# Carrying per-pixel reciprocal deviations over a DRAM scratch, with square and norm on GpSimd

## The chip, the cores and the metric

The kernel runs on one core of a Trainium2 chip, as one launch. The metric is the device time of the whole program in microseconds. Before the change the median of three runs is 893.47 us (891.79 to 895.72).

## The reference

The input is x of shape (8, 64, 64, 64), batch, channel, row, column, in float32. Two blocks follow each other.

```
# block one: four scans; each line is the line before it, convolved over 9 taps and all channels
new = cur + relu(row_conv(prev, K))         # down, up, right, left

# block two
pooled = x.mean((2, 3)); hdn = layernorm(pooled @ w_fc1.T); dyn = hdn @ w_fc2.T   # a 5x5 filter per image and channel
out = depthwise_conv(x, dyn)                                    # 25 taps, zero padding
u = out.mean(1); s2 = square(out - u).mean(1)                   # over the 64 channels of a pixel
out = (out - u) * rsqrt(s2 + EPS); out = ln2_w * out + ln2_b
out = gelu(einsum(out, w_expand))                               # 64 -> 256 channels
gx = sqrt(sum(square(out), (2, 3))); nx = gx / (gx.mean(1) + EPS)
out = gamma * (out * nx) + beta + out
out = einsum(out, w_shrink) + x                                 # 256 -> 64 channels
```

## The kernel before

The function `scans` is block one. It keeps one line of all eight images on chip at a time and runs TensorE, VectorE and GpSimd in a serial chain, and it fills the first 500 us. Only two lines of it touch the change: it prepares the constants `pick` (L398, L399) and `spread` (L361 to L364), the second by one ScalarE copy.

The function `block_two` is block two. The image rows are folded on the partitions: partition c holds channel c of the even rows, partition 64 + c the same channel of the odd rows. An image is cut into two halves, so there are 16 units of 128 partitions by 16 row pairs by 64 columns, 1024 elements a partition.

Each engine has its own written-out order of instructions, a loop over slots s from -1 to 20, and the engines meet only through semaphores. In slot s:

- TensorE convolves unit s + 1 (`convolve`, L1043), in six pieces of five matmuls, into one of two pairs of PSUM banks. Five of the 15 tap pairs are its work. It also sums unit s - 1 over the channels (`statistics`, L1066), spreads the reciprocal deviations of unit s - 2 from rows of subtotals to all channels (`widen`, L1080, twice, each for half of the unit), expands that unit (`expand`, L1090, four times) and shrinks unit s - 5 (`shrink`, L1112, twice). `respond` (L1103) takes a mean over channels once for an image.
- VectorE adds ten taps of unit s onto the convolved sums in PSUM (`take_tap`, L872); the last one writes `inner` in SBUF. Between the taps stand `norm` (L902) of unit s - 2, `make_var` and `make_rstd` (L886, L896) of unit s - 1, `finish` (L932) of unit s - 5 and, once for an image, `sum_energy` and `respond` (L911, L915).
- ScalarE makes five products of unit s + 1 with its taps (`product`, L754), the square of `inner` (`square`, L766), the root of the variance (`root`, L779), the gelu of unit s - 2 (`gelu`, L791) and the sums of its squares (`add_squares`, L798).
- GpSimd sums the products into `part` (`add_product`, L711) and adds `part` to `inner` (`add_inner`, L718), splits the image for TensorE (`split_low`, L701) and builds the filter matrices of the next image (`make_dyn`, L724).
- SyncE issues the transfers: the rows that a tap needs from the other half of the partitions (`cross`, L670) and the stores of the output (`store`, L680).

`expand` waits for the gelu before it, since both use the one pair of banks `exp_ps`. A `statistics` writes the bank `stat_ps`, which `widen` uses as well. After the last taps (slot 16 and on) only expansion, gelu, shrinking and stores are left.

Of the kernel before, what the change touches and what calls it, by code (L numbers as in the profile page):

```python
# [64 lines left out]
def build(nc, x, k_td, k_dt, k_lr, k_rl, fc1, ln1_w, ln1_b, fc2, ln2_w, ln2_b,  # L65
          expand, shrink, gamma, beta, out):
    with ExitStack() as ctx:
# [4 lines left out]
        def sb(name, shape, dt=F32):  # L72
# [8 lines left out]
            pick=sb("pick", [P, 32 + 2 * SUBS - 2]),  # L81
# [10 lines left out]
            spread=sb("spread", [P, 4 * SUBS, P]),  # L92
# [6 lines left out]
def scans(nc, bank, kept, x, kernels, fc1, ln1_w, ln1_b, fc2, ln2_w, ln2_b,  # L99
# [6 lines left out]
    with ExitStack() as ctx:  # L106
# [181 lines left out]
        def _(act):  # L288
# [55 lines left out]
            with act.Fori(0, counts[1] // UNROLL) as i:  # L344
                for u in range(UNROLL):
# [15 lines left out]
            rows = ident[:, :].rearrange("p (g k) -> p g k", k=32)[:, :, 0:2 * SUBS].rearrange("p g (k a) -> p g k a", a=1)  # L361
            act.wait_ge(ident_ready, 1)
            act.activation(kept["spread"][:, :, :].rearrange("p (g j) (k c) -> p g (j k) c", j=SUBS, c=C),
                           rows.to_broadcast([P, 4, 2 * SUBS, C]), ACT.Copy)  # L364

# [4 lines left out]
        def _(dve):  # L370
# [25 lines left out]
            def prepare_constants():  # L396
                dve.wait_ge(consts, 1)
                dve.memset(kept["pick"][0:C, 2 * SUBS - 2:2 * SUBS - 1], 1.0 / C)  # L398
# [152 lines left out]
def block_two(nc, psum, kept, out):  # L551
# [4 lines left out]
    with ExitStack() as ctx:  # L556
# [10 lines left out]
        INNERS = 3  # L567
# [15 lines left out]
        normed = sb("normed", [P, 2, COLS])  # L583
# [17 lines left out]
        tap_lo = sb("tap_lo", [P, B, len(PE_TAPS), 2], F32R)  # L601

# [27 lines left out]
        wide_done = sem("wide_done")  # L630
# [29 lines left out]

        def out_bank(k):
            return out_ps if k < 4 * (B - 1) else psum[:, 4 + k % 4, :]
# [4 lines left out]
        def _(sp):  # L667
# [27 lines left out]
        def _(pool):  # L695
# [38 lines left out]

            pool.wait_ge(taps_known, 1)
            pool.wait_ge(dyn_ready, 1)
            for u in range(UNITS):
                for n in range(1, N_ACT):
                    add_product(u, n)
                if u + 2 < UNITS:  # L740
                    split_low(u + 2)
                if u % 2 == 0 and u // 2 + 1 < B:
                    make_dyn(u // 2 + 1)
                add_inner(u)

        @block.scalar
        def _(act):
# [18 lines left out]
            def square(u):  # L766
                act.wait_ge(inner_ready, u + 1)
                if u > 0:
                    act.wait_ge(stats_done, u)
                if u > 1:  # L770
                    act.wait_ge(energy_ready, 2 * (u - 1))
                act.activation(squares[:, :], inner[:, u % INNERS, :, :].rearrange("p j w -> p (j w)"),  # L772
                               ACT.Square).then_inc(squared, 1)

# [16 lines left out]
            def gelu(u, c, m):  # L791
                act.wait_ge(exp_done, 2 * (2 * u + c) + m + 1)
                if m == 0 and u >= WIDE:
                    act.wait_ge(out_done, 2 * (u - WIDE) + c + 1)
                act.activation(wide[:, m, :, u % WIDE, c * COLS:(c + 1) * COLS], exp_ps[:, :, :],  # L795
                               ACT.Gelu, bias=expand_bias[:, m:m + 1]).then_inc(gelu_done, 1)

            def add_squares(u, m):  # L798
                b, h = u // 2, u % 2
                act.wait_ge(gelu_done, 4 * (u + 1))  # L800
# [4 lines left out]
                if m == 0 and u + 1 < UNITS:  # L805
                    act.wait_ge(stats_done, u + 2)
                act.activation(squares[:, :].bitcast(BF16).rearrange("p (a n) -> p a n", a=2),
# [15 lines left out]
            for s in SLOTS_RUN:  # L823
                w, e, v = s - 1, s - 2, s - 5

                def products(lo, hi):
                    if s + 1 < UNITS:
                        for n in range(lo, min(hi, N_ACT)):
                            product(s + 1, (n + 1) % N_ACT)

                if 2 <= s + 2 < UNITS:
                    split_high(s + 2)
                for i in range(4):
                    if e in range(UNITS):
                        gelu(e, i // 2, i % 2)
                    products(i, i + 1)
                    if i == 1 and w in range(UNITS):
                        square(w)
                products(4, N_ACT)
# [3 lines left out]
                if 0 < e <= UNITS and e % 2 == 0:  # L843
                    root_energy(e // 2 - 1)
                if e in range(UNITS):
                    add_squares(e, 0)
                    add_squares(e, 1)

        @block.vector
        def _(dve):  # L850
# [21 lines left out]
            def take_tap(u, i):  # L872
# [6 lines left out]
                if i == N_DVE - 1 and u >= INNERS:  # L879
                    dve.wait_ge(normed_ready, 2 * (u - INNERS + 1))  # L880
# [15 lines left out]
            def make_rstd(u):  # L896
                dve.wait_ge(std_ready, u + 1)
                if u > 1:
                    dve.wait_ge(wide_done, 2 * (u - 1))
                dve.reciprocal(rstd[:, u % 2, :], std[:, :]).then_inc(rstd_ready, 1)  # L900

            def norm(u, c):  # L902
                k = 2 * u + c
                dve.wait_ge(wide_done, k + 1)
                if k >= 2:
                    dve.wait_ge(exp_done, 2 * k - 2)
                dve.tensor_tensor(normed[:, c, :],
                                  inner[:, u % INNERS, c * CROWS:(c + 1) * CROWS, :].rearrange("p j w -> p (j w)"),
                                  stat_ps[:, :], ALU.mult).then_inc(normed_ready, 1)
# [5 lines left out]
            def respond(b):  # L915
                n = RESP_STEPS * b
                dve.wait_ge(resp_mean, b + 1)
                dve.tensor_scalar(resp[:, 2, 0:1], out_ps[:, 0:1], EPS, None, ALU.add).then_inc(resp_step, 1)
# [62 lines left out]
            for s in SLOTS_RUN:  # L981
                w, e, v = s - 1, s - 2, s - 5
# [8 lines left out]
                if e in range(UNITS):  # L991
                    norm(e, 0)
                take(1)
# [3 lines left out]
                if e in range(UNITS):  # L997
                    norm(e, 1)
                take(2)
                if v >= 0:  # L1000
                    finish(v, 1)
                if 0 < e <= UNITS and e % 2 == 0:
                    sum_energy(e // 2 - 1)
                take(2)
# [6 lines left out]
                if 0 < e <= UNITS and e % 2 == 0:  # L1011
                    respond(e // 2 - 1)
# [3 lines left out]
        def _(pe):  # L1016
# [49 lines left out]
            def statistics(u):  # L1066
                pe.wait_ge(squared, u + 1)
                if u > 0:
                    pe.wait_ge(normed_ready, 2 * u)
                flat = inner[:, u % INNERS, :, :].rearrange("p j w -> p (j w)")  # L1070
                for n, image in enumerate((flat, squares)):
                    for k in range(SUBS):
                        for g in range(4):
                            at = (g * SUBS + k) * STAT_COLS
                            mm = pe.matmul(stat_ps[32 * g:32 * g + 32, n * STAT_COLS:(n + 1) * STAT_COLS],
                                           kept["pick"][:, 2 * (SUBS - 1 - k):2 * (SUBS - 1 - k) + 32],
# [3 lines left out]
            def widen(u, c):  # L1080
                pe.wait_ge(rstd_ready, u + 1)
                if c > 0:
                    pe.wait_ge(normed_ready, 2 * u + c)
                per = 2 * SUBS
                for g in range(per):
                    mm = pe.matmul(stat_ps[:, g * STAT_COLS:(g + 1) * STAT_COLS], kept["spread"][:, per * c + g, :],  # L1086
                                   rstd[:, u % 2, :], start=True, stop=True)
                mm.then_inc(wide_done, 1)

            def expand(u, c, m):  # L1090
                e = 2 * (2 * u + c) + m
                if m == 0:
                    pe.wait_ge(normed_ready, 2 * u + c + 1)
                if e > 0:
                    pe.wait_ge(gelu_done, e)
                else:
                    pe.wait_ge(weights_ready, 1)
                for hp in range(2):
                    half = slice(C * hp, C * hp + C)
                    mm = pe.matmul(exp_ps[:, hp, :], expand_w[half, m, :], normed[half, c, :], start=True, stop=True)  # L1100
                mm.then_inc(exp_done, 1)

            def respond(b):  # L1103
                pe.wait_ge(resp_root, b + 1)
                if b > 0:
                    pe.wait_ge(finished, 4 * b)
                for m in range(HALVES):
                    mm = pe.matmul(out_ps[:, 0:1], kept["mean_ce"][:, :].to_broadcast([P, P]), resp[:, 1, m:m + 1],
# [17 lines left out]
            for s in SLOTS_RUN:  # L1126
                u, w, e, v = s + 1, s - 1, s - 2, s - 5
# [5 lines left out]
                def at_w(stage, *which):  # L1133
                    if w in range(UNITS):
                        stage(w, *which)

                def at_e(stage, *which):
                    if e in range(UNITS):
                        stage(e, *which)

                def at_v(stage, *which):
                    if v >= 0:
                        stage(v, *which)

                at_e(widen, 0)
                at_v(shrink, 0)
                at_e(expand, 0, 0)
                conv(0)
                at_e(widen, 1)
                at_e(expand, 0, 1)  # L1150
                at_v(shrink, 1)
                at_e(expand, 1, 0)
                conv(1)
                at_e(expand, 1, 1)
                conv(2)
                at_w(statistics)
                conv(3)
                conv(4)
                if 0 < e <= UNITS and e % 2 == 0:
                    respond(e // 2 - 1)  # L1160
                conv(5)

# [25 lines left out]
```

## Time and profile before

| | |
|---|---|
| median of three runs | 893.47 us |
| the profiled execution | 893.85 us |
| its span | 892.0 us |
| TensorE matmuls | 816.9 us, 92% of the span |
| VectorE | 604.4 us, 68% |
| GpSimd | 454.5 us, 51% |
| ScalarE | 433.2 us, 49% |
| mean granted TensorE clock | 0.97 of full speed |

The page cuts the span into 40 slices; two of its lines show the two blocks. The busy shares over the whole span are a mean over both, and block two (from the 23rd slice on) has other shares than block one.

```
PE   5999999999999999999999675889999999999775
ACT  5690005777750000000000154798989898988662
```

A time in the answers is counted from the start of the span. "busy" is the time of the instructions, and an idle time is put down to the instruction that ended it.

### The profile page before, as it was taken

How to read it: one execution, taken by the hardware profiler on the slowest of the kernel's cores; microseconds unless marked ns; L12 is line 12 of the kernel's file. 1: busy time of each engine (PE TensorE's matmuls, PEld its weight loads, DVE VectorE, ACT ScalarE, POOL GpSimd, SP SyncE). 2: the span in 40 equal slices, each digit the busy share in tenths (PEclk: the TensorE clock that was granted, in tenths of full speed). 3: DMA queues.
4: the chain of work that ended last, by engine and by line, in shares of the span. 5: the costliest groups of instructions: out<-in, count | busy, mean ns of one | idle time of the engine just before them, and what ended most of it. 6: DMA issues, size and time to landing. Idle time of an engine off the chain costs nothing. (4 is left out here: it accounts for less than half of the span.)

```text
span 892.0 us, 16129 instructions
## 1 busy us (share of the span) xinstructions
PE 816.9 (92%) x5639; PEld 666.5 (75%) x5639; DVE 604.4 (68%) x1127; ACT 433.2 (49%) x520; POOL 454.5 (51%) x443
## 2 busy tenths in 40 slices
PE   5999999999999999999999675889999999999775
PEld 5999999999999999999999654455454555545231
DVE  4666666666666666678888657777887778888722
ACT  5690005777750000000000154798989898988662
POOL 2333333333323333368888466767777776765500
PEclk9999999999999999999999788889999999999997
DMA  6750000000000000000000100110222222223123
GB/s 139 170 141 0 0 0 1 0 0 0 0 1 1 0 0 0 1 1 0 0 0 0 47 0 24 34 36 24 48 47 47 47 47 47 47 47 71 24 48 71
DMA packets 51189, 26.99 MB, mean 30 GB/s; under 512 B 40720, under 2 KB 49104, under 8 KB 51152
## 3 DMA queue, kind: packets, MB, share of 16 engines
q1 hardware_dynamic: 51152, 26.51, 13.2%
q8 instruction: 22, 0.36, 0.2%
q14 instruction: 15, 0.12, 0.0%
HBM read 9.98 MB, written 8.39 MB: 21 GB/s over the span
## 5 line engine op out<-in xcount | busy, mean ns | idle before, releaser
L487 PE MATMUL psum<-line_hi,taps_hi 128*128 128x256 f32 x1270 | 203.0, 292 | 11.8 <-DVE taps_lo L383 8.6
L501 PE MATMUL psum<-line_lo,taps_hi 128*128 128x256 f32 x1270 | 202.5, 291 | 0.8 <-DVE line_lo L436 0.8
L495 PE MATMUL psum<-line_hi,taps_lo 128*128 128x256 f32 x1270 | 202.0, 291 | 0.0
L436 DVE SCALAR_TENSOR_TENSOR line_lo<-psum,rest 128x256 fp32r<-128x256 f32 x254 | 108.2, 426 | 123.6 <-POOL rest L263 115.3
L487 PEld LDWEIGHTS psum<-line_hi,taps_hi 128*128 128x128 f32 x1270 | 177.1, 192 | 13.0 <-issue 9.3
L501 PEld LDWEIGHTS psum<-line_lo,taps_hi 128*128 128x128 f32 x1270 | 176.4, 191 | 2.0 <-DVE line_lo L436 1.8
L495 PEld LDWEIGHTS psum<-line_hi,taps_lo 128*128 128x128 f32 x1270 | 176.7, 191 | 0.0
L263 POOL TENSOR_TENSOR rest<-x,line_hi 128x256 f32<-128x256 f32 x127 | 82.9, 653 | 168.5 <-DVE line_hi L427 168.5
L709 POOL TENSOR_TENSOR part<-part,prod 128x960 f32<-128x960 f32 (+2 forms) x64 | 145.2, 2269 | 24.3 <-ACT part L764 17.5
L315 ACT ACTIVATE by_h<-x (+1 forms) x128 | 85.7, 670 | 106.1 <-DVE x L416 104.5
L263 POOL TENSOR_TENSOR rest<-by_h,line_hi 128x256 f32<-128x256 f32 x127 | 91.5, 721 | 83.4 <-DVE line_hi L427 83.4
L416 DVE TENSOR_TENSOR x<-line_hi,line_lo 128x256 f32 (+1 forms) x190 | 105.5, 555 | 0.2
L883 DVE SCALAR_TENSOR_TENSOR psum<-x,tap_all,psum 128x930 f32<-128x930 f32 (+2 forms) x80 | 96.7, 1209 | 1.3
L1100 PE MATMUL psum<-normed,expand_w 64*128 64x512 f32 x256 | 75.0, 663 | 22.6 <-ACT wide L795 17.1
L764 ACT ACTIVATE prod<-x,tap_all 128x960 f32<-128x960 f32 (+2 forms) x64 | 70.1, 1101 | 37.5 <-POOL part L709 30.1
L883 DVE SCALAR_TENSOR_TENSOR psum<-crossed,tap_cross,psum 128x992 f32<-128x992 f32 (+1 forms) x64 | 80.7, 1261 | 10.3 <-PE psum L1060 9.4
L722 POOL TENSOR_TENSOR inner<-inner,part 128x1024 f32<-128x1024 f32 x16 | 37.9, 2367 | 86.5 <-DVE inner L883 86.5
L795 ACT ACTIVATE wide<-psum,expand_bias 128x1024 f32<-128x1024 f32 x64 | 70.9, 1109 | 20.9 <-PE psum L1100 20.7
L1060 PE MATMUL psum<-x_hi,dyn_hi 128*128 128x512 f32 x160 | 70.3, 439 | 9.1 <-DVE inner L883 5.8
L751 ACT ACTIVATE x_hi<-x 128x1024 fp32r<-128x1024 f32 x16 | 16.7, 1051 | 126.2 <-PEq L106 121.7
L1121 PE MATMUL psum<-wide,shrink_now 128*64 128x512 f32 x256 | 67.1, 653 | 3.7 <-DVE shrink_now L928 2.9
L427 DVE SCALAR_TENSOR_TENSOR line_hi<-psum,x 128x256 fp32r<-128x256 f32 x127 | 54.0, 425 | 21.9 <-PE psum L487 8.6
(129 smaller groups left out, 899.3 us busy)
## 6 DMA issues: line engine op xcount, KB each, us to landing
stage<-in_x_dram SPq DMA_DIRECT2D x32, 256.0 KB, 4.1
out_dram<-x SPq DMA_DIRECT2D x32, 256.0 KB, 4.4
crossed<-x SPq DMA_DIRECT2D x16, 256.0 KB, 3.5
crossed<-x SPq DMA_DIRECT2D x16, 240.0 KB, 3.6
fc_in<-in_L_conv_w_fc_dram SPq DMA_DIRECT2D x2, 100.0 KB
taps<-in_L_conv_k_td_dram SPq DMA_DIRECT2D x2, 80.0 KB, 3.3
taps<-in_L_conv_k_dt_dram SPq DMA_DIRECT2D x2, 80.0 KB, 3.3
taps<-in_L_conv_k_lr_dram SPq DMA_DIRECT2D x2, 80.0 KB, 3.5
```

The lines of the kernel that those rows point to most:

```text
L263: pool.tensor_tensor(rest[:, slot % 2, :].rearrange("p (b i) -> p b i", b=B), x_line, line_hi[:, (slot + 1) % SLOTS, :, REACH:REACH + WP]. ...
L315: act.activation(dst, src, ACT.Copy).then_inc(turned, 1)
L416: dve.tensor_tensor(kept_line(s, row_of(s, k)), line_hi[:, made, :, part].bitcast(F32), line_lo[:, made, :, part].bitcast(F32), ALU.add).t ...
L436: dve.scalar_tensor_tensor(out=line_lo[:, (slot + 1) % SLOTS, :, part], in0=as_lines(line_ps[slot][:, 0:LINE]), scalar=0.0, in1=as_lines(r ...
L487: mm = pe.matmul(line_ps[slot][:, 0:LINE], taps_hi[:, s, d, :], line_hi[:, slot, :, d:d + WP], start=(d == 0), stop=(d == OFFSETS - 1))
L495: pe.matmul(line_ps[slot][:, 0:LINE], taps_lo[:, s, d, :], line_hi[:, slot, :, d:d + WP], start=False, stop=False, skip_group_check=True)
L501: mm = pe.matmul(line_ps[slot][:, 0:LINE], taps_hi[:, s, d, :], line_lo[:, slot, :, d:d + WP], start=False, stop=(d == OFFSETS - 1), skip_ ...
L709: pool.tensor_tensor(dst, dst, other, ALU.add).then_inc(part_step, 1)
L795: act.activation(wide[:, m, :, u % WIDE, c * COLS:(c + 1) * COLS], exp_ps[:, :, :], ACT.Gelu, bias=expand_bias[:, m:m + 1]).then_inc(gelu_ ...
L883: dve.scalar_tensor_tensor(out=dst, in0=src, scalar=weight, in1=here, op0=ALU.mult, op1=ALU.add).then_inc(tap_step, 1)
L1060: mm = pe.matmul(conv_ps[:, 2 * (u % 2) + c, :], weight[:, b % 2, n, :, :].rearrange("p o c -> p (o c)"), image[:, u % 2, CROWS * c:CROWS ...
L1100: mm = pe.matmul(exp_ps[:, hp, :], expand_w[half, m, :], normed[half, c, :], start=True, stop=True)
```

## The change

The products on ScalarE become four and the taps on VectorE eleven: the tap ("up", 3) moves. `widen` and the constant `spread` go. In their place SyncE stores the reciprocal deviations of a unit in DRAM and reads them back twice, each time broadcast to 64 partitions, into `rstd_wide`. `square` moves from ScalarE to GpSimd, and `norm` from VectorE to GpSimd, one instruction for a unit where there were two. `inner` has two buffers in place of three, `normed` holds two whole units. `add_squares` writes to a buffer of its own, `dump`. The expansion goes by channel halves first (m) and image halves second (c), and for the last two units it uses three pairs of banks. The order of the slots changes on all engines.

```
-            ("down", 3), ("cross", 2)]
+            ("down", 3), ("up", 3), ("cross", 2)]
-SIDES = [("up", 1), ("down", 1), ("up", 3)]
+SIDES = [("up", 1), ("down", 1)]
-        INNERS = 3
+        INNERS = 2
+        EXP_SETS = 3
+        FREE_CONV = 4 * (UNITS - 2)
+        def exp_set(e):
+            first = 4 if e < FREE_CONV else (4, 0, 2)[(e - FREE_CONV) % EXP_SETS]
+            return psum[:, first:first + 2, :]
# SyncE
+            def spread_rstd(u):
+                sp.wait_ge(rstd_ready, u + 1)
+                if u > 1:
+                    sp.wait_ge(rstd_spread, 32 * (u - 1))
+                sp.dma_start(rstd_dram[u % 2], rstd[:, u % 2, :]).then_inc(rstd_stored[u % 2], 16)
+                sp.wait_ge(rstd_stored[u % 2], 16 * (u // 2 + 1))
+                if u > 0:
+                    sp.wait_ge(normed_ready, u)
+                rows = rstd_dram[u % 2].rearrange("(g q) n -> g (q n)", g=4)
+                for h in range(2):
+                    mine = rows[:, SUBS * h * STAT_COLS:SUBS * (h + 1) * STAT_COLS].rearrange("(a g) n -> a g n", a=1)
+                    sp.dma_start(rstd_wide[C * h:C * h + C, :].rearrange("p (g n) -> p g n", g=4),
+                                 mine.to_broadcast([C, 4, SUBS * STAT_COLS])).then_inc(rstd_spread, 16)
             for s in SLOTS_RUN:
+                if s - 1 in range(UNITS):
+                    spread_rstd(s - 1)
+                if s >= 5:
+                    store(s - 5)
                 if s + 2 < UNITS:
                     cross(s + 2)
-                if s >= 5:
-                    store(s - 5)
# GpSimd
+            def square(u):
+                pool.wait_ge(inner_ready, u + 1)
+                if u > 0:
+                    pool.wait_ge(stats_done, u)
+                pool.tensor_tensor(squares[:, :], image, image, ALU.mult).then_inc(squared, 1)
+            def norm(u):
+                pool.wait_ge(rstd_spread, 32 * (u + 1))
+                if u > 1:
+                    pool.wait_ge(exp_done, 4 * (u - 1))
+                pool.tensor_tensor(normed[:, u % 2, :], image, rstd_wide[:, :], ALU.mult).then_inc(normed_ready, 1)
-            for u in range(UNITS):
-                (add_product x4, split_low, make_dyn, add_inner of unit u)
+            for s in range(UNITS + 2):
+                w, e = s - 1, s - 2
+                if w in range(UNITS):
+                    add_inner(w)
+                    square(w)
+                if e >= 0:
+                    norm(e)
+                if s < UNITS:
+                    for n in range(1, N_ACT):
+                        add_product(s, n)
+                if s + 2 < UNITS:
+                    split_low(s + 2)
+                if s % 2 == 0 and s // 2 + 1 < B:
+                    make_dyn(s // 2 + 1)
# ScalarE, in a slot (n = s - 3)
+                add_squares(n, 1); split_high(s + 2); product(s + 1, 0)
+                square_mean(w); root(w)
+                if n in range(UNITS) and n % 2 == 1: root_energy(n // 2)
+                gelu(e, 0, 0); product(s + 1, 1); product(s + 1, 2); gelu(e, 0, 1); add_squares(e, 0)
+                gelu(e, 1, 0); product(s + 1, 3); gelu(e, 1, 1)
# VectorE, in a slot
+                take(2); finish(v, 0); take(2)
+                if n in range(UNITS) and n % 2 == 1: sum_energy(n // 2)
+                make_var(w); take(1); make_rstd(w); take(1); finish(v, 1); take(1)
+                if n in range(UNITS) and n % 2 == 1: respond(n // 2)
+                take(N_DVE)
# TensorE, in a slot
+                shrink(v, 0); conv(0); conv(1); statistics(w); expand(e, 0, 0); shrink(v, 1)
+                conv(2); expand(e, 0, 1); conv(3)
+                if n in range(UNITS) and n % 2 == 1: respond(n // 2)
+                expand(e, 1, 0); conv(4); conv(5); expand(e, 1, 1)
```

The lists of the three engines are written here one call after the other; in the kernel each stands under the test that its unit exists. `expand` now waits for the gelu before it only up to the last two units.

## Rows read from the trace of the kernel before

**Rows 1.** Timeline of GpSimd, `add_inner`: start us, us, engine, line, operation [idle before].
```profile
537.88 2.37 POOL L722 TENSOR_TENSOR inner<-inner,part 128x1024 f32<-128x1024 f32 x1 [3.13 <-DVE inner L883]
...
619.55 2.37 POOL L722 TENSOR_TENSOR inner<-inner,part 128x1024 f32<-128x1024 f32 x1 [5.31 <-DVE inner L883]
...
639.38 2.38 POOL L722 TENSOR_TENSOR inner<-inner,part 128x1024 f32<-128x1024 f32 x1 [5.95 <-DVE inner L883]
...
660.17 2.37 POOL L722 TENSOR_TENSOR inner<-inner,part 128x1024 f32<-128x1024 f32 x1 [4.63 <-DVE inner L883]
...
822.65 2.36 POOL L722 TENSOR_TENSOR inner<-inner,part 128x1024 f32<-128x1024 f32 x1 [9.02 <-DVE inner L883]
838.82 2.35 POOL L722 TENSOR_TENSOR inner<-inner,part 128x1024 f32<-128x1024 f32 x1 [4.33 <-DVE inner L883]
```

**Rows 2.** Windows: stretch, length, busy of PE, PEld, DVE, ACT, POOL, clock, DMA.
```profile
639.39:802.00 162.61, 154.50 (x900) 84.46 (x896) 130.39 (x161) 147.73 (x157) 116.85 (x57) 1.00 0.24 52
```

**Rows 3.** Groups by form, 640 to 802 us: busy us, mean ns | idle before, releaser.
```profile
L722 POOL TENSOR_TENSOR inner<-inner,part 128x1024 f32<-128x1024 f32 x9 | 21.4, 2374 | 48.3 <-DVE inner L883 48.3
...
L704 POOL TENSOR_TENSOR x_lo<-x,x_hi 128x1024 fp32r<-128x1024 f32 x8 | 16.0, 2005 | 0.0
...
L907 DVE TENSOR_TENSOR normed<-inner,psum 128x512 f32<-128x512 f32 x16 | 10.9, 680 | 0.0
...
L900 DVE RECIPROCAL rstd<-std 128x128 f32<-128x128 f32 x8 | 7.6, 953 | 0.0
...
L891 DVE TENSOR_TENSOR var<-psum,mean_sq 128x128 f32<-128x128 f32 x8 | 2.3, 292 | 30.4 <-ACT mean_sq L777 30.4
```

**Rows 4.** Groups of the page, whole span: a cross tap and a gelu.
```profile
L883 DVE SCALAR_TENSOR_TENSOR psum<-crossed,tap_cross,psum 128x992 f32<-128x992 f32 (+1 forms) x64 | 80.7, 1261 | 10.3 <-PE psum L1060 9.4
...
L795 ACT ACTIVATE wide<-psum,expand_bias 128x1024 f32<-128x1024 f32 x64 | 70.9, 1109 | 20.9 <-PE psum L1100 20.7
```

**Rows 5.** Timeline of one slot, 700 to 722 us.
```profile
705.78 1.94 PE L1121 MATMUL psum<-wide,shrink_now 128*64 128x512 f32 x8
...
707.65 1.13 PE L1100 MATMUL psum<-normed,expand_w 64*128 64x512 f32 x4
...
708.71 0.51 PE L1060 MATMUL psum<-x_hi,dyn_lo 128*128 128x512 f32 x1
...
713.40 0.64 PE L1075 MATMUL psum<-inner,pick 128*32 128x128 f32 x16
...
714.41 0.50 PE L1060 MATMUL psum<-x_hi,dyn_hi 128*128 128x512 f32 x1
...
715.46 1.28 ACT L783 ACT_TABLE_LOAD   x1
...
718.20 1.16 PE L1086 MATMUL psum<-rstd,spread 128*128 128x128 f32 x8
```

**Rows 6.** Timeline of TensorE: groups that began after an idle time.
```profile
578.23 2.07 PE L1100 MATMUL psum<-normed,expand_w 64*128 64x512 f32 x4 [1.86 <-DVE normed L907]
585.61 1.13 PE L1100 MATMUL psum<-normed,expand_w 64*128 64x512 f32 x4 [1.31 <-ACT wide L795]
```

**Rows 7.** Windows of 1 us: the granted clock stands before the last two numbers.
```profile
580.00:581.00 1.00, 1.00 (x4) 0.67 (x3) 0.96 (x2) 0.99 (x2) 1.00 (x2) 0.50 0.70 234
```

**Rows 8.** Timeline of a slot with `respond`, 818 to 822 us.
```profile
818.33 0.60 PE L1108 MATMUL psum<-resp,mean_ce 128*128 128x1 f32 x4 [0.25 <-ACT resp L789]
...
820.18 0.15 DVE L918 TENSOR_SCALAR resp<-psum 128x1 f32<-128x1 f32 x1
...
821.24 1.27 DVE L883 SCALAR_TENSOR_TENSOR inner<-crossed,tap_cross,psum 128x1024 f32<-128x1024 f32 x1
```

**Rows 9.** DMA issues: operation, count, KB each, us to landing.
```profile
crossed<-x SPq DMA_DIRECT2D x16, 256.0 KB, 3.5
```

**Rows 10.** Timeline of the end: the last sum of squares, the last shrinking.
```profile
870.92 1.91 ACT L807 ACTIVATE squares<-wide 128x2048 bf16<-128x2048 f32 x1
...
876.33 9.91 PE L1121 MATMUL psum<-wide,shrink_now 128*64 128x512 f32 x32 [1.23 <-DVE shrink_now L928]
```

More of the change, by code:

```diff
@@ L823, in _ @@
             for s in SLOTS_RUN:
[L824 to L829, printed above, removed]
+                w, e, n = s - 1, s - 2, s - 3
+                if n in range(UNITS):
+                    add_squares(n, 1)
                 if 2 <= s + 2 < UNITS:
                     split_high(s + 2)
[L833 to L839, printed above, removed]
+                if s + 1 < UNITS:
+                    product(s + 1, 0)
                 if w in range(UNITS):
@@ L842, in _ @@
                     root(w)
[L843 to L847, printed above, removed]
+                if n in range(UNITS) and n % 2 == 1:
+                    root_energy(n // 2)
+                for i, between in enumerate(((1, 2), (), (3,), ())):
+                    if e in range(UNITS):
+                        gelu(e, i // 2, i % 2)
+                    if i == 1 and e in range(UNITS):
+                        add_squares(e, 0)
+                    for p in between:
+                        if s + 1 < UNITS:
+                            product(s + 1, p)
         @block.vector
@@ L989, in take @@
                     taken[0] += n
-                if e in range(UNITS):
-                    norm(e, 0)
-                take(1)
+                take(2)
                 if v >= 0:
@@ L996, in _ @@
                 take(2)
[L997 to L1004, printed above, removed]
+                if n in range(UNITS) and n % 2 == 1:
+                    sum_energy(n // 2)
                 if w in range(UNITS):
@@ L1010, in _ @@
                 take(1)
-                if 0 < e <= UNITS and e % 2 == 0:
-                    respond(e // 2 - 1)
+                if v >= 0:
+                    finish(v, 1)
+                take(1)
+                if n in range(UNITS) and n % 2 == 1:
+                    respond(n // 2)
                 take(N_DVE)
@@ L1075, in statistics, with expand @@
                             mm = pe.matmul(stat_ps[32 * g:32 * g + 32, n * STAT_COLS:(n + 1) * STAT_COLS],
-                                           kept["pick"][:, 2 * (SUBS - 1 - k):2 * (SUBS - 1 - k) + 32],
+                                           kept["pick"][:, SUBS - 1 - k:SUBS - 1 - k + 32],
                                            image[:, at:at + STAT_COLS], start=(k == 0), stop=(k == SUBS - 1))
                 mm.then_inc(stats_done, 1)
[L1080 to L1094, printed above, removed]
+            def expand(u, m, c):
+                e = 4 * u + 2 * m + c
+                if e == 0:
+                    pe.wait_ge(weights_ready, 1)
+                if c == 0 and m == 0:
+                    pe.wait_ge(normed_ready, u + 1)
+                if e == FREE_CONV + 1:
+                    pe.wait_ge(tap_step, N_DVE * UNITS)
+                if 0 < e <= FREE_CONV:
                     pe.wait_ge(gelu_done, e)
-                else:
-                    pe.wait_ge(weights_ready, 1)
+                elif e >= FREE_CONV + EXP_SETS:
+                    pe.wait_ge(gelu_done, e - EXP_SETS + 1)
                 for hp in range(2):
                     half = slice(C * hp, C * hp + C)
-                    mm = pe.matmul(exp_ps[:, hp, :], expand_w[half, m, :], normed[half, c, :], start=True, stop=True)
+                    mm = pe.matmul(exp_set(e)[:, hp, :], expand_w[half, m, :], normed[half, u % 2, c * COLS:(c + 1) * COLS],
+                                   start=True, stop=True)
                 mm.then_inc(exp_done, 1)
@@ L1131, in conv, with at_e, at_v @@
                         convolve(u, piece)
[L1133 to L1137, printed above, removed]
+                def at_e(m, c):
                     if e in range(UNITS):
-                        stage(e, *which)
-                def at_v(stage, *which):
+                        expand(e, m, c)
+                def at_v(c):
                     if v >= 0:
[L1143 to L1147, printed above, removed]
+                        shrink(v, c)
+                at_v(0)
                 conv(0)
[L1149 to L1152, printed above, removed]
                 conv(1)
-                at_e(expand, 1, 1)
+                if w in range(UNITS):
+                    statistics(w)
+                at_e(0, 0)
+                at_v(1)
                 conv(2)
-                at_w(statistics)
+                at_e(0, 1)
                 conv(3)
+                if n in range(UNITS) and n % 2 == 1:
+                    respond(n // 2)
+                at_e(1, 0)
                 conv(4)
-                if 0 < e <= UNITS and e % 2 == 0:
-                    respond(e // 2 - 1)
                 conv(5)
+                at_e(1, 1)
 _INS = ['x', 'L0_conv_k_td', 'L0_conv_k_dt', 'L0_conv_k_lr', 'L0_conv_k_rl', 'L1_conv_w_fc1', 'L1_conv_ln1_w',
```

70 lines of the change are left out of this document (23 added, 47 removed).

## The prediction

> **What bounds the kernel now.** First the slices of the page: block two begins at about 500 us, and the change touches nothing before it but a ScalarE copy that lies in an idle stretch. Then the timeline of `add_inner`, which GpSimd starts when VectorE has finished the taps of a unit, so the distance of two of them is a slot [rows 1]. A slot with an odd number takes 639.38 - 619.55 = 19.83 us, an even one, which also carries `respond`, 660.17 - 639.38 = 20.79. Slots 1 to 4 take 81.67 us, slots 5 to 14 203.10 (five odd, five even), slot 15, the last with taps, 16.17, and what follows 892.0 - 838.82 = 53.2.
>
> Next the windows of eight steady slots (162.6 us) [rows 2]. For one slot of 20.3 us TensorE is busy 19.3, ScalarE 18.5, VectorE 16.3, GpSimd 14.6. Two engines are nearly full. VectorE idles 3.8 us a slot in one place, where `make_var` waits for the squared mean [rows 3]: the square of `inner` stands in the middle of ScalarE's list and `statistics` behind it on TensorE. So the period is a loop through all four engines, and not one engine's sum.
>
> **The change, part by part, for one steady slot.**
>
> TensorE: `widen` goes, two groups of eight, 1.16 us each with the last one's tail [rows 5], about 1.05 without it; 19.3 becomes 17.2. ScalarE loses a product (1.1) and the square (1.0): 16.4. VectorE loses two `norm` (0.68 each [rows 3]) and gains a tap (1.26 [rows 4]): 16.2. GpSimd loses an addition (2.2 to 2.37, as `inner`'s) and gains a square and a norm. The trace has no multiplication of two full images on GpSimd; the nearest row is its addition of the same 128 by 1024 shape, 2.37 us [rows 3]. I take 2.37 for each. Bounds: 2.0 (the subtraction of `split_low`, same shape [rows 3]) and 3.1 (a third over the addition). That makes 14.6 - 2.3 + 4.7 = 17.0. The four engines now stand at 16.2 to 17.2, so the sums alone would allow 17.2; what follows is the walk through the waits.
>
> Walk, with time 0 where VectorE starts the taps of slot s and GpSimd its list 0.14 later. Starts that follow each other on one engine are a little closer than the durations, and I use these: shrink 1.87, expand 1.07 (the steps 705.78, 707.65, 708.71), fifteen convolution matmuls in 718.20 - 714.41 = 3.79, so 1.26 a piece, statistics 1.01 [rows 5]; tap 1.25 and gelu 1.1 [rows 4], `add_squares` 1.9 [rows 10], reciprocal 0.95 [rows 3], and `finish`, of `norm`'s size but with a third operand, 0.72.
> - GpSimd: inner until 2.5, square until 4.8, norm until 7.2.
> - TensorE: the pieces 0 and 1 of the convolution are done before 4.8, or at 5.5 where TensorE comes late; statistics until 5.9 (6.5); expand from 7.2 to 8.3, shrink to 10.1, piece 2 to 11.4, expand to 12.5, piece 3 to 13.75, then `respond` in even slots, expand, pieces 4 and 5, done at 17.5 to 17.8, and the last expand until 18.9.
> - ScalarE: squared mean at 6.2 (6.8), table load 1.28 [rows 5], root until 7.9 (8.4), table load, first gelu from 9.7 to 10.9, two products to 12.9, gelu to 14.0 (TensorE's third expand waits for it, 0.2 us), `add_squares` to 15.9, gelu to 17.0, product, gelu after the last expand.
> - VectorE: two taps, `finish`, two taps until 5.8; variance at 6.3 (6.8) instead of after a wait of 3.8 us; then two taps, reciprocal, `finish`, a tap: 12.6; the last four taps take 4.9.
>
> *Odd slots.* VectorE is through at 17.4, and TensorE's convolution, which gates the next taps, at 17.5. But TensorE now idles from 2.9 to 4.9, since it has come to `statistics` before GpSimd has the square. After an idle 1.86 us the first group of four took 2.07 us in place of 1.13, after 1.31 us it did not [rows 6], and two microseconds behind the first the granted clock is 0.50, the lower level, 1.2 GHz [rows 7]. Idle here is about 1.95 us, so I take the fall: statistics takes 1.8, the variance starts at 7.0, and the slot ends at 17.9 (17.4 without it). Against 19.83 that is 1.9.
>
> *Even slots.* VectorE comes to `respond` at 12.8, but TensorE makes the mean only behind piece 3, at 14.35 (13.75 and 0.60). In the trace TensorE starts it at 818.33 and VectorE, which had other work, spends 821.24 - 820.18 = 1.06 us on its five small steps before the next tap [rows 8]. So VectorE waits 1.5 us: 14.4, 15.5, and four taps: 20.4. Against 20.79 that is 0.4. This wait is what takes the place of the old one: behind it on VectorE stand four taps, and GpSimd and the convolution after next wait for these.
>
> *The scratch.* In slot s - 1 the reciprocal is ready at 9.6; GpSimd comes to the norm at 17.9 + 4.8 = 22.7. Between lie three transfers on SyncE's queue, one after the other and two together. The trace has no store to a scratch; the nearest row is the shifted copy, 256 KB in 3.5 us [rows 9]. With issues of 0.6 each I take 3.6 + 4.2 = 7.8 us; bounds 4 (half a copy for each hop) and 12 (the copies behind one another and behind a store). It is hidden by 5 us in the steady part and costs in full in the tail. The Trainium skill, page "DMA: Bandwidth & Descriptors", section "Anatomy of one DMA — SWDGE (gpsimd) path", has 2.0 us of fixed cost for each transfer, most of it the receipt of the write, and bytes over 436 GB/s. No run here shows a store of 64 KB; by the page, as an estimate, the bounce would be 2.15 + 3.2 = 5.4 us, and the tail 2.4 us shorter than I make it.
> SyncE's wait for `rstd_ready` stands ahead of `store` and `cross`. The store goes behind the second `finish` (11.6) anyway, `cross` behind the last tap, with a slot to land in: nothing.
>
> *Start.* Slot 0 has only taps: +1.2. Slots 1 to 4: the first ends at 16.6 by VectorE (variance at 6.3, seven taps, reciprocal), the second and third at 17.75 (no shrink yet, TensorE reaches the third expand before its gelu, and pieces 4 and 5 end at 17.7), slot 4 at 20.0 (`respond` behind piece 3 at 13.9). Together 72.1 against 81.67: -9.6.
>
> *Slots 5 to 14.* 5 x 17.9 + 5 x 20.4 = 191.5 against 203.1: -11.6.
>
> *Slot 15.* No convolution, so the slot was short before; the new order has eleven taps and the wait for GpSimd's square at the lower clock: 17.95 against 16.17: +1.8.
>
> *Tail.* Before, 876.33 - 838.82 = 37.5 us lie between the start of slot 16 and the last shrinking, 3.4 of it behind the last sum of squares (870.92, 1.91 and 0.1 to read its result) [rows 1, 10]. Now: reciprocal at 9.6, bounce to 17.4, norm to 19.8, expand at the lower clock to 21.9, gelu, shrink and expand to 26.3, gelu, one `add_squares`, two gelus until 31.5, the last `add_squares` to 33.4, and 3.4: 36.8. The three pairs of banks save about what the scratch costs: -0.7.
>
> Sum: +1.2 - 9.6 - 11.6 + 1.8 - 0.7 = -18.9. On the profiled execution, 893.85, that is 874.95; this one lies 0.4 above the median, so 874.6 there. I say 875.
>
> **The rivals.**
>
> A. *TensorE is the last everywhere.* The lower clock also holds through the first expand of even slots, or GpSimd's square and norm take 2.8 each. For it: the first expand is reached by a chain of three GpSimd instructions at 7.2 with nothing to spare. Against: the idle before it is 0.7 to 1.3 us, and 1.31 kept the clock [rows 6]. 0.8 us later in each slot: pairs of 39.6 us instead of 40.6, -5 in slots 5 to 14, -6.4 in 1 to 4, the rest as above (+2.3): -9.1, so 884.8.
>
> B. *The clock stays, and the scratch is fast.* Odd slots end at 17.4 (-2.6 in all), and each hop takes under 3 us, -2.5 in the tail: 869.8.
>
> C. *ScalarE takes the gain.* Its two table loads, the root and the gelus form a chain that must start behind `statistics`; if each gelu is reached about 1.5 us later than in my walk, the third expand waits for it and the pieces behind it too. For it: the third expand already waits 0.2 us. Against: ScalarE's sum falls by 2.1. Pairs stay at 40.6, slots 1 to 4 give 4, the rest +2.3: 892.
>
> D. *Slower: the scratch comes late.* From the reciprocal at 9.6 of one slot to the tap behind the next convolution there are the bounce, norm 2.4 and 10.6 of TensorE; two slots last at least 22.6 us and the bounce. With a bounce over 18 us a pair is longer than the 40.6 of before: broadcasting one 4 KB piece of DRAM to 64 partitions would have to crawl, or stand behind stores. At 19.5 us: pairs of 42.1, +7.5 in slots 5 to 14, +3 in slots 1 to 4, +12 in the tail, +3 in slots 0 and 15: 919. Nothing in the row of 3.5 us speaks for it.
>
> That the change does not do what it says would mean that VectorE still waits at the variance; only with the square late on GpSimd, which is A.
>
> **How the numbers follow.** Forecast 0.50, A 0.18, B 0.17, C 0.10, D 0.05. The predicted time is that of the forecast. Two in ten may be left out: D, most of C, and a little of B and A; 866 to 887. No change here means within 0.5%, 889.0 to 897.9, which is about what a measurement of this kernel tells apart: C and little else, 0.09. Slower: D and the worst of C, 0.06. Faster 0.85.
>
> **What would show it.** Distances of `add_inner` near 17.9 and 20.4 in turn; the idle before `make_var` down from 3.8 us to under 1.5; a new idle on VectorE of about 1.5 us ahead of `respond` in even slots, put down to TensorE; clock 0.50 behind `statistics` in odd slots only; the norm on GpSimd never waiting for a transfer before slot 17, and there for about 10 us. The forecast is wrong if even slots are as short as odd ones, if GpSimd waits for `rstd_wide` in the steady part, or if the square takes 3 us or more.

## The result, and the profile after

The changed kernel takes 888.32 us, median of nine runs (884.66 to 889.81), against 893.44 us before. The ratio is 0.9932, 95% interval 0.9915 to 0.9949. The profiled execution took 888.81 us with a span of 887.1. It is faster, as forecast, but by 0.7% where 2.1% were forecast, and 888.3 lies outside the range of 866 to 887.

The timeline of GpSimd in the changed kernel, `add_inner` (now L744; start us, us), shows from slot 8 on slots in turn of 23.5 (even) and 17.6 us (odd), where 20.8 and 19.8 stood before [rows 1]. Slot 5 takes 19.55 and slot 7 16.86:

```profile
539.73 2.37 POOL L744 TENSOR_TENSOR inner<-inner,part 128x1024 f32<-128x1024 f32 x1 [8.25 <-DVE inner L910]
...
697.44 2.38 POOL L744 TENSOR_TENSOR inner<-inner,part 128x1024 f32<-128x1024 f32 x1 [5.33 <-DVE inner L910]
...
715.04 2.37 POOL L744 TENSOR_TENSOR inner<-inner,part 128x1024 f32<-128x1024 f32 x1 [1.96 <-DVE inner L910]
...
738.50 2.38 POOL L744 TENSOR_TENSOR inner<-inner,part 128x1024 f32<-128x1024 f32 x1 [5.33 <-DVE inner L910]
...
797.04 2.37 POOL L744 TENSOR_TENSOR inner<-inner,part 128x1024 f32<-128x1024 f32 x1 [1.86 <-DVE inner L910]
...
817.73 2.36 POOL L744 TENSOR_TENSOR inner<-inner,part 128x1024 f32<-128x1024 f32 x1 [6.64 <-DVE inner L910]
836.56 2.35 POOL L744 TENSOR_TENSOR inner<-inner,part 128x1024 f32<-128x1024 f32 x1 [5.20 <-DVE inner L910]
```

Slot 14 (797.04 to 817.73) is even too, and takes only 20.69. The groups by form, 640 to 802 us, say what is dear in the others (busy us, mean ns | idle before):

```profile
L762 POOL TENSOR_TENSOR squares<-inner 128x1024 f32<-128x1024 f32 x8 | 15.2, 1895 | 0.6
...
L946 DVE TENSOR_TENSOR shrink_now<-shrink_t,resp 128x128 f32<-128x128 f32 x4 | 5.2, 1308 | 0.1
...
L943 DVE TENSOR_SCALAR resp<-resp 128x2 f32<-128x2 f32 x4 | 4.8, 1193 | 0.1
...
L940 DVE SCALAR_TENSOR_TENSOR resp<-resp,gamma 128x2 f32<-128x2 f32 x4 | 3.4, 850 | 0.1
...
L918 DVE TENSOR_TENSOR var<-psum,mean_sq 128x128 f32<-128x128 f32 x8 | 2.3, 292 | 6.8 <-ACT mean_sq L810 6.8
...
L938 DVE RECIPROCAL resp<-resp 128x1 f32<-128x1 f32 x4 | 0.7, 164 | 0.1
L936 DVE TENSOR_SCALAR resp<-psum 128x1 f32<-128x1 f32 x4 | 0.6, 158 | 6.6 <-PE psum L1116 6.6
```

The wait at the variance went from 3.8 to 0.85 us a slot [rows 3], and the new wait ahead of `respond` is 1.65 us, both as forecast. But three of the five steps of `respond`, on 2 or 128 elements a partition, take 0.85, 1.19 and 1.31 us. Before the change the same view gave them 221, 170 and 293 ns. GpSimd's timeline of the same even slot suggests a cause, which the experiments test; first VectorE, then GpSimd:

```profile
688.60 0.16 DVE L938 RECIPROCAL resp<-resp 128x1 f32<-128x1 f32 x1
688.80 0.89 DVE L940 SCALAR_TENSOR_TENSOR resp<-resp,gamma 128x2 f32<-128x2 f32 x1
689.73 1.19 DVE L943 TENSOR_SCALAR resp<-resp 128x2 f32<-128x2 f32 x1
690.95 1.31 DVE L946 TENSOR_TENSOR shrink_now<-shrink_t,resp 128x128 f32<-128x128 f32 x1
```

```profile
687.67 2.00 POOL L726 TENSOR_TENSOR x_lo<-x,x_hi 128x1024 fp32r<-128x1024 f32 x1
689.63 1.26 POOL L753 TENSOR_TENSOR dyn_hi<-ident_half,tap_hi 128x640 fp32r<-128x640 f32 x1
690.86 1.26 POOL L753 TENSOR_TENSOR dyn_lo<-ident_half,tap_lo 128x640 fp32r<-128x640 f32 x1
```

Each slow step ends when a GpSimd instruction ends: 689.69 and 689.67, 690.92 and 690.89, 692.26 and 692.12. By then GpSimd has begun its next instruction, and the next step waits for that one. In slot 14 GpSimd has no image to split and no filters to build; its list is through, and the same three steps take their old times:

```profile
811.80 0.22 DVE L940 SCALAR_TENSOR_TENSOR resp<-resp,gamma 128x2 f32<-128x2 f32 x1
812.05 0.17 DVE L943 TENSOR_SCALAR resp<-resp 128x2 f32<-128x2 f32 x1
812.25 0.29 DVE L946 TENSOR_TENSOR shrink_now<-shrink_t,resp 128x128 f32<-128x128 f32 x1
```

The theory (called L in the experiments) is that VectorE and GpSimd exclude each other at SBUF for these forms of instruction. The Trainium skill states it: page "SBUF — State Buffer", section "SBUF: two separate sides", has a port pair shared by the two and held for a whole instruction, by any GpSimd operation, and on VectorE by one in a two-port mode or, against a GpSimd operation that reads SBUF, by one with two SBUF inputs. The rival (M) is that the steps are slow because of the scratch's transfers, or because a wait is counted as busy time.

### The profile page after: what moved, and what is told of

Its sections match the earlier page's. It is cut to its first block and busy times, and to the rows that moved or that the text cites. A ratio compares the mean times of both kernels' runs of the same rounds, so it can differ in the third digit from the quotient of the medians.

```text
span 887.1 us, 15588 instructions
## 1 busy us (share of the span) xinstructions
PE 797.9 (90%) x5383; PEld 643.8 (73%) x5383; DVE 620.0 (70%) x1111; ACT 399.6 (45%) x485; POOL 485.9 (55%) x459
## 5 line engine op out<-in xcount | busy, mean ns | idle before, releaser
L731 POOL TENSOR_TENSOR part<-part,prod 128x960 f32<-128x960 f32 (+2 forms) x48 | 108.6, 2262 | 20.9 <-ACT prod L806 16.0
L910 DVE SCALAR_TENSOR_TENSOR psum<-x,tap_all,psum 128x930 f32<-128x930 f32 (+3 forms) x96 | 116.4, 1213 | 1.7
L1107 PE MATMUL psum<-normed,expand_w 64*128 64x512 f32 x256 | 77.3, 686 | 23.3 <-POOL normed L769 11.7
L1073 PE MATMUL psum<-x_hi,dyn_hi 128*128 128x512 f32 x160 | 72.7, 455 | 24.5 <-DVE inner L910 21.1
L744 POOL TENSOR_TENSOR inner<-inner,part 128x1024 f32<-128x1024 f32 x16 | 38.0, 2372 | 61.4 <-DVE inner L910 61.4
L1073 PEld LDWEIGHTS psum<-x_hi,dyn_hi 128*128 128x128 f32 x160 | 33.1, 207 | 52.2 <-DVE inner L910 26.3
L1073 PE MATMUL psum<-x_lo,dyn_hi 128*128 128x512 f32 x160 | 70.1, 438 | 0.0
```

What stands on the lines that cost most here:

```text
L731: pool.tensor_tensor(dst, dst, other, ALU.add).then_inc(part_step, 1)
L910: dve.scalar_tensor_tensor(out=dst, in0=src, scalar=weight, in1=here, op0=ALU.mult, op1=ALU.add).then_inc(tap_step, 1)
L1073: mm = pe.matmul(conv_ps[:, 2 * (u % 2) + c, :], weight[:, b % 2, n, :, :].rearrange("p o c -> p (o c)"), image[:, u % 2, CROWS * c:CROWS ...
L1107: mm = pe.matmul(exp_set(e)[:, hp, :], expand_w[half, m, :], normed[half, u % 2, c * COLS:(c + 1) * COLS], start=True, stop=True)
```

## Experiments

**1. `respond` with its operands in PSUM.** Same five steps in the same places; gamma is copied once to two spare columns. `...` stands for what is left out of a line.

```
+            at = 2 * STAT_COLS + 8 + HALVES * i          # resp_ps(i): columns of the statistics bank
-  scalar_tensor_tensor(out=resp[:, 4, :], in0=resp[:, 1, :], ..., in1=kept["gamma"][:, :], ...)
-  tensor_scalar(resp[:, 5, :], resp[:, 4, :], 1.0, None, ALU.add)
-  tensor_tensor(shrink_now, kept["shrink_t"], resp[:, 5, :]..., ALU.mult)
+  scalar_tensor_tensor(out=resp_ps(1), in0=resp[:, 1, :], ..., in1=resp_ps(0), ...)
+  tensor_scalar(resp_ps(2), resp_ps(1), 1.0, None, ALU.add)
+  tensor_tensor(shrink_now, kept["shrink_t"], resp_ps(2)..., ALU.mult)
```

> The changed kernel with the operands of VectorE's respond in PSUM: gamma, the product and the sum with 1 lie in spare columns of the statistics bank, so that no step of it has two SBUF inputs or goes from SBUF to SBUF. Theory L (port): in the changed kernel three of the five steps took 0.85, 1.19 and 1.31 us on the mean where they took 0.22, 0.17 and 0.29 before, because VectorE stands still until the GpSimd instruction in flight has ended; with PSUM operands they go back to 0.15 to 0.35 each, even slots shrink from 23.5 to about 20.8 us, and the program by about 7 slots of 2.7 us: 866 to 873. Theory M (the steps are slow for the DMA traffic of the scratch or for a wait that the profile counts as busy): they stay near 1 us, time unchanged at 888.

Measured: 871.42 us, ratio to before 0.9752 (0.9723 to 0.9781). The groups by form, 640 to 802 us:

```profile
L950 DVE TENSOR_TENSOR shrink_now<-shrink_t,psum 128x128 f32<-128x128 f32 x5 | 1.4, 288 | 0.2
L944 DVE SCALAR_TENSOR_TENSOR psum<-resp,psum 128x2 f32<-128x2 f32 x5 | 1.1, 224 | 0.2
...
L940 DVE TENSOR_SCALAR resp<-psum 128x1 f32<-128x1 f32 x5 | 0.8, 158 | 8.2 <-PE psum L1121 8.2
```

The steps are back at 0.29 and 0.22 us, the even slots 8, 10 and 12 take 20.7 (slot 6 takes 21.0, slot 4 22.6), and 16.9 us are gained on the changed kernel. The scratch's transfers and the waits between the steps are all still there. Slot 14, where nothing was stalled, keeps its time (20.75 and 20.69), so PSUM operands as such give nothing. So M does not hold.

**2. TensorE's `respond` one place earlier**, ahead of `expand(e, 0, 1)` and piece 3.

> The changed kernel with TensorE's respond one place earlier, behind piece 2 of the convolution instead of behind the expand and piece 3. The mean then comes about 2.3 us earlier, before VectorE reaches its respond. My step 'VectorE waits 1.5 us there' says: the idle before VectorE's respond goes from 1.65 to near 0 and even slots from 23.5 to about 21.9; if the port theory holds, the three slow steps may come out longer or shorter, depending on which GpSimd instructions they now meet (they are then beside the additions of products). 876 to 882. The rival, that the wait for TensorE is not on the path: 888.

Measured: 879.99 us, 0.9847 (0.9821 to 0.9874). The wait is gone (no idle ahead of the first step), and even slots take 22.2. The three steps came out longer, 0.72, 1.93 and 1.31 us on the mean: in all 0.6 us more than in the changed kernel. The first one still meets an addition of products, but it is the middle one that grows, since it now meets the 2.00 us of `split_low` (first VectorE, then GpSimd):

```profile
682.87 0.72 DVE L940 SCALAR_TENSOR_TENSOR resp<-resp,gamma 128x2 f32<-128x2 f32 x1
683.62 1.94 DVE L943 TENSOR_SCALAR resp<-resp 128x2 f32<-128x2 f32 x1
```

```profile
683.53 2.00 POOL L726 TENSOR_TENSOR x_lo<-x,x_hi 128x1024 fp32r<-128x1024 f32 x1
```

Not all odd slots gained: 7 and 9 take 18.5 where they took 16.9 and 17.6, and slot 13 takes 19.6 for 17.5, each with a stretch of the granted clock at 0.50.

**3. Both.**

> Both edits. Theory L and the TensorE wait are separate terms: even slots about 19.2 us, odd 17.6, and then TensorE or ScalarE is last in the slot: 858 to 866. If the one hides the other, no better than the better of the two alone.

Measured: 858.3 us, 0.9603 (0.9576 to 0.9629); even slots 18.97, odd 16.90. `respond` in an even slot, VectorE's timeline:

```profile
675.86 0.15 DVE L940 TENSOR_SCALAR resp<-psum 128x1 f32<-128x1 f32 x1
676.04 0.16 DVE L942 RECIPROCAL resp<-resp 128x1 f32<-128x1 f32 x1
676.24 0.22 DVE L944 SCALAR_TENSOR_TENSOR psum<-resp,psum 128x2 f32<-128x2 f32 x1
676.50 0.17 DVE L947 TENSOR_SCALAR psum<-psum 128x2 f32<-128x2 f32 x1
676.71 0.29 DVE L950 TENSOR_TENSOR shrink_now<-shrink_t,psum 128x128 f32<-128x128 f32 x1
```

The step from one input to one output, now from PSUM to PSUM, takes 0.17 beside a running GpSimd instruction. The two edits save 8.3 us (experiment 2) and 16.9 (experiment 1) alone, and 30.0 together, more than the 25.2 of the sum. Two reasons can be read off the traces of the runs: the earlier place alone lengthens the stalls by 0.6 us in an even slot, and its odd slots 7 and 9 take 18.5 where they take 16.9 here. This is the fastest version, 35 us under the kernel before.

**4 to 7. Work put beside `respond` in the kernel before.** There GpSimd idles 4.6 us ahead of `add_inner` in even slots [rows 1]. The work is on a tile that nothing needs any more (`fc2_t`, here `spare`), and nothing uses its results. The cut leaves out a memset of `spare` ahead of the loop.

```
                     make_dyn(u // 2 + 1)
+                if u % 2 == 0:
+                    for i in range(3):                   # 5 in the second kernel
+                        pool.wait_ge(idle_work, 3 * (u // 2) + i)
+                        pool.tensor_tensor(spare, spare, spare, ALU.mult).then_inc(idle_work, 1)
+                        # third and fourth kernel: pool.memset(spare, 0.0), 10 and 6 times
                 add_inner(u)
```

> The kernel before, with three idle multiplications of 128 by 512 elements (about 1.2 us each) added to GpSimd's list in even units, ahead of add_inner, where GpSimd was idle for 4.6 us. They take part in nothing. Theory L: they now run beside VectorE's respond, whose three steps grow from 0.2 to 0.3 us to 0.6 to 1.3 us each, even slots grow by 1.5 to 2.7 us, the program by 10 to 20 us: 903 to 913. Theory M, and the view that idle time of GpSimd is free: unchanged at 893.

Measured: 896.04 us, ratio 1.0031 (1.0021 to 1.0041), less than I expected: only one step was caught, and the even slots 6 to 12 take 21.3, 0.5 longer. (The profiled execution was the shortest of ten, 892.34.) The multiplications (736.29, 3.28 us for three) end at 739.57; VectorE's timeline:

```profile
738.85 0.73 DVE L931 SCALAR_TENSOR_TENSOR resp<-resp,gamma 128x2 f32<-128x2 f32 x1
739.61 0.17 DVE L934 TENSOR_SCALAR resp<-resp 128x2 f32<-128x2 f32 x1
739.82 0.29 DVE L937 TENSOR_TENSOR shrink_now<-shrink_t,resp 128x128 f32<-128x128 f32 x1
```

> The kernel before with five idle multiplications in even units where b_fill_read had three. There the three took 3.28 us and ended at 739.57, and of VectorE's respond only the first of the three steps with SBUF operands met them: it began at 738.85 and ended at 739.58 (0.73 us for 0.22), the two behind it kept 0.17 and 0.29. Theory L: with two more instructions of 1.09 us, all three steps meet one each and end with it: about 0.7, 1.1 and 1.1 us, 2.2 us more than before; even slots about 23 us, the program 905 to 912. Theory M, or 'one stall only': 0.7 us once, 896.

Measured: 901.95 us, 1.0098 (1.0072 to 1.0124), under the 905 to 912 expected; the even slots 6 to 12 take 22.0. Under five multiplications, 743.58 to 749.11:

```profile
746.15 0.73 DVE L931 SCALAR_TENSOR_TENSOR resp<-resp,gamma 128x2 f32<-128x2 f32 x1
746.92 0.17 DVE L934 TENSOR_SCALAR resp<-resp 128x2 f32<-128x2 f32 x1
747.12 1.01 DVE L937 TENSOR_TENSOR shrink_now<-shrink_t,resp 128x128 f32<-128x128 f32 x1
```

Two of three were caught, and the 2.2 us I had reckoned were 1.2: the middle step got in between two GpSimd instructions. I had taken it that VectorE always loses the next turn; it does so in the changed kernel and did not here. One difference is that each filler waits on a semaphore for the one before it, which `split_low` and `make_dyn` do not; whether that is the reason no run tests.

> The same place filled with ten memsets of 512 elements, which write SBUF and read nothing. If VectorE is held by any GpSimd instruction that uses SBUF, the three steps (0.22, 0.17, 0.29 us) grow by up to one memset each; if only by one that reads, they keep their times and the program its 893 (or a little more, should the memsets reach past the time at which GpSimd would take up add_inner).

Measured: 902.07 us, 1.0098 (1.0081 to 1.0115), but most of it because the ten memsets reach past the time of `add_inner`: even slots take 21.85, 1.06 more than before, of which the stall is 0.44. First GpSimd, then VectorE:

```profile
742.54 5.78 POOL L752 MEMSET fc_t<- 128x512 f32 x10
...
745.15 0.22 DVE L931 SCALAR_TENSOR_TENSOR resp<-resp,gamma 128x2 f32<-128x2 f32 x1
745.40 0.61 DVE L934 TENSOR_SCALAR resp<-resp 128x2 f32<-128x2 f32 x1
746.05 0.29 DVE L937 TENSOR_TENSOR shrink_now<-shrink_t,resp 128x128 f32<-128x128 f32 x1
```

Beside memsets, which write a tile and read none, the two steps with two SBUF inputs are free, and the step with one input from SBUF to SBUF is held until 746.01, the end of the sixth memset (742.54 + 6 x 0.578). So there are two kinds of collision.

> b_fill_write with six memsets where it had ten. The ten took 5.78 us and reached to 748.32, past the time at which GpSimd took up add_inner, so that 902 holds a late add_inner as well as the stall. Six of 0.58 us end about 0.1 to 0.6 us behind the start of VectorE's fourth step and leave GpSimd idle before add_inner. Theory L as b_fill_write left it (a memset holds only the step from SBUF to SBUF with one input, 0.61 us for 0.17, and not the two steps with two inputs): even slots 20.8 to 21.3 us, the program 894 to 897.

Measured: 894.61 us, 1.0018 (1.0009 to 1.0028). That step took 0.61 us in two of the four even slots of the window and 0.17 in the others (mean 390 ns); the slots with the stall are 21.2 us long, those without 20.8. The stall alone makes the difference of 0.44.

**8. The way over DRAM made longer**: the store of the reciprocals is done twice, one after the other.

> The changed kernel with the store of the reciprocals done twice, one behind the other, so that the way over DRAM takes about 2 us longer (a store lands in 1.5 us). My step 'hidden by about 5 us in the steady part, in full in the tail': the norm still waits for no transfer before slot 17, and there about 2 us longer; 888 to 892. Rival D (the scratch is on the path): 2 us a slot, 915 to 920.

Measured: 890.25 us, 0.9965 (0.995 to 0.9979). The steady slots did not change (23.44 and 17.46). GpSimd waits once for a transfer, in the tail, 11.6 us where it waited 9.8. So the scratch is hidden in the steady part, with room for the 2 us added.

**9. One pair of banks to the end** (`FREE_CONV = 4 * UNITS`).

> The changed kernel without the three pairs of banks for the last two units (expand waits for the gelu before it, as it does earlier). I reckoned that the pairs save in the tail about what the way over DRAM costs there, some 3 to 6 us: 889 to 894. If TensorE and ScalarE are not last there, no difference: 888.

Measured: 887.03 us, 0.9933 (0.9917 to 0.995), against 888.32 (884.66 to 889.81) for the changed kernel. From the last `add_inner` to the end both profiled executions take 50.5 us, so the three pairs of banks save nothing.

## Why the prediction was wrong, step by step

The step that failed is in *Even slots*: "VectorE, which had other work, spends 821.24 - 820.18 = 1.06 us on its five small steps before the next tap". The row is read rightly, but it comes from a slot where GpSimd idles beside these steps: the idle of 9.02 us ahead of 822.65 [rows 1, 8] says so. The prediction's walk of GpSimd stops at the norm, 7.2 us into the slot. In the new order the additions, `split_low` and `make_dyn` follow, and they last to about 18 us into an even slot (692.1 in the slot that began at 673.98). VectorE begins `respond` 14.4 us into it, as forecast, and so meets them. From the first of the five steps at 688.40 to the next tap at 692.18 it took 3.8 us, 2.7 more than the 1.06 reckoned. The sum has no term for such a meeting: it was priced at nothing, without a reason. The rule of the Trainium skill, page "SBUF — State Buffer", section "SBUF: two separate sides", would have given one for the steps with two SBUF inputs. The taps, which have one operand in PSUM, do keep their 1.25 us.

By slots, measured against forecast from the profiled executions: even slots 6, 8, 10 and 12 +3.05 each, slot 4 +3.6, slot 14 +0.3, together +16.1. The rest nearly cancels, in part by luck: slot 0 +0.65, slots 1 to 3 -1.3, slot 5 +1.65 (it is as long in experiment 1), slot 7 -1.0, slots 9, 11 and 13 -1.0 together, slot 15 +0.9, tail -2.0. The sum is about +13.9 on 874.95, and 888.81 was measured. With the stall taken out (experiment 1) the time is 871.4, 3.6 under the forecast.

Of slot 4's +3.6 the stall is only 1.2. There TensorE's second expand waited for the first gelu, the mean came late, and VectorE stood still for it:

```profile
602.36 1.17 PE L1107 MATMUL psum<-normed,expand_w 64*128 64x512 f32 x4 [2.61 <-ACT wide L828]
606.64 0.16 DVE L936 TENSOR_SCALAR resp<-psum 128x1 f32<-128x1 f32 x1 [3.56 <-PE psum L1116]
```

- *Squares and norm on GpSimd at 2.37 each.* Norm right (2.38). The square took 1.90, below my lower bound of 2.0; what that saved no run isolates.
- *The wait for TensorE at `respond`, 1.5 us.* Right in the steady part: 1.65, and 8.3 us for the program when it was taken away alone.
- *The lower clock in odd slots, 0.5 us each.* About right in size, wrong in place, and not in every odd slot. I had TensorE idle ahead of `statistics`; with the longer even slots it idled 2.20 us ahead of the convolution, and 1.5 us later its matmuls went from 0.40 to 0.61 us, while the windows gave a clock of 0.50, that is 1.2 GHz:

```profile
697.35 0.50 PE L1073 MATMUL psum<-x_hi,dyn_hi 128*128 128x512 f32 x1 [2.20 <-DVE inner L910]
...
698.88 0.61 PE L1073 MATMUL psum<-x_hi,dyn_hi 128*128 128x512 f32 x1
...
700.00:702.00 2.00, 0.92 (x6) 0.20 (x9) 1.97 (x3) 1.00 (x1) 2.00 (x2) 0.50 0.24 84
```

  The odd slots 9, 11 and 13 begin with such an idle (2.20 to 2.26 us) and take 17.5 to 17.6. In experiment 1 it is gone, the clock stays in these three slots, and they take 16.87. So about 0.7 us in each of the three is a second effect of the stall. Slot 7 began with 1.90 us of idle and its clock fell too, but for under 4 us where it fell for about 7 in the others, and it takes 16.86. I took the fall from the length of one idle time (1.86 us against 1.31 [rows 6]), and experiment 1 shows that this does not decide it. Its slots 7 and 9 have the same idle of 1.38 us ahead of `statistics` and of 1.24 or 1.25 ahead of the expand; in slot 7 the clock fell and the expand took 2.08 us, in slot 9 it stayed:

```profile
655.97 0.65 PE L1093 MATMUL psum<-inner,pick 128*32 128x128 f32 x16 [1.38 <-POOL squares L766]
658.29 2.08 PE L1112 MATMUL psum<-normed,expand_w 64*128 64x512 f32 x4 [1.24 <-POOL normed L773]
...
695.12 0.64 PE L1093 MATMUL psum<-inner,pick 128*32 128x128 f32 x16 [1.38 <-POOL squares L766]
697.45 1.13 PE L1112 MATMUL psum<-normed,expand_w 64*128 64x512 f32 x4 [1.25 <-POOL normed L773]
```

  What does decide it stays open.
- *The scratch, 7.8 us from the reciprocal to the norm.* Right: 845.06 to 853.04 for the last unit, 8.0 us. Its parts were other than mine (1.5 for the small store, 5.4 for the two broadcasts, which run together). The figure of the Trainium skill, page "DMA: Bandwidth & Descriptors", section "Anatomy of one DMA — SWDGE (gpsimd) path", gave 5.4 us by my estimate for the whole way, which is too short; that section is about transfers that GpSimd issues, and these are SyncE's.
- *Tail: the three pairs of banks save about what the scratch costs.* Wrong in its reason: the pairs save nothing (experiment 9). The tail was 2.0 us shorter than forecast for reasons that no run here isolates.
- *Rivals.* A's 884.8 is 3.5 us from the measured time and C's 892 3.7, but neither is what happened. (A's own 0.8 us a slot on 17.9 + 20.4 makes pairs of 39.9, not 39.6.) For A, the square and the norm did not take 2.8, and the clock stayed full in the even slots 6 to 14. C's wait of TensorE for the gelu is 0.25 us a slot in the steady part, as in the walk; only in slot 4 was it large. B asked for the full clock and for hops under 3 us; the clock fell, and the broadcasts took 5.4. D is excluded by experiment 8.

## What to carry to other kernels

When work moves to GpSimd, list VectorE's instructions that will run beside it and look at their operands, the smallest ones too: here the three that read two SBUF tiles, or went from SBUF to SBUF by `tensor_scalar`, lasted until about the end of the GpSimd instruction in flight where they took 0.2 to 0.3 us alone (beside a memset only the `tensor_scalar` did). A duration read from a row holds only for what the other engine did at that time, so check what ran beside it before using it. If such steps must stay on the path, put their operands in PSUM; here that was worth 16.9 us, more than three times the change itself.

## What the runs showed of the hardware

- A VectorE step on 2 elements a partition took 0.17 us alone and 1.94 beside `split_low` on GpSimd, which took 2.00 (experiment 2). The profile counts the stall as busy time, so it appears in no list of waits; only the mean of the group gives it away.
- There are two kinds of collision. A step with two SBUF inputs collides with a GpSimd instruction that reads SBUF (0.73 for 0.22), and not with a memset (0.22). A `tensor_scalar` from SBUF to SBUF with one input collides with a memset too (0.61 for 0.17). The reciprocal from SBUF to SBUF (0.16) and the steps of experiments 1 and 3 with a PSUM operand (0.17 to 0.29) did not collide. The rule of the Trainium skill, page "SBUF — State Buffer", section "SBUF: two separate sides", agrees with the steps of two inputs. That the `tensor_scalar` ran in a two-port mode, and why the reciprocal is free, no run here shows.
- GpSimd multiplies a tile of 1024 elements a partition with itself in 1.90 us, and two different tiles in 2.38.
